# Second and third layer norm of a decoder layer: one square root a pair of tiles on ScalarE, reciprocal and refining step on VectorE

## The chip, the cores and the metric

The kernel runs on one core of a Trainium2 chip. The metric is the device time of one execution in microseconds (us); lower is better. The time before is 491.82 us, the median of 3 runs (491.54 to 492.5).

## What is computed

One decoder layer on x of 4 x 256 tokens and 512 features, in fp32, with a context of 4 x 64 tokens. Each of three blocks ends in a layer norm without weights:

```
layernorm(x) = (x - mean(x)) / sqrt(var(x) + 1e-5)          # over the 512 features

x = layernorm(x + gelu(x @ ((w1.T @ w2.T) * sparse_mask) + b2))
x = layernorm(x + cross_attention(x, ctx))                   # 32 query heads, 8 key/value heads, width 128, rotary positions
x = layernorm(x + (x @ W.T + b) + lora(x))                   # 8 experts of rank 16, weighted per batch by a softmax
```

The router that weights the experts takes the mean of the tokens 107 to 254 of the second norm's output, one row of logits per batch.

## The kernel before

The 1024 tokens are 8 tiles of 128 tokens (X[:, t, :], t = 0 to 7), the tokens on the partitions. Products are taken in three fp32r matmuls each: every operand is split into a high part (a copy on ScalarE, the helpers that end in `_hi`, L801) and a low part (the difference, on VectorE, L1139, or GpSimd, the helpers that end in `_lo`).

Cross attention runs over the 8 key/value heads g (LAST = 7), each with 4 query heads. A head has four units u; `scores`, `mask_scores`, `row_max`, `shift`, `exps`, `row_sum`, `row_inverse`, `probs` (GpSimd, L1728), `probs_transpose`, `pt_hi` and `pt_lo` are the steps of a unit's softmax in that order, over TensorE, VectorE, ScalarE and GpSimd. `value_out(g, n, b)` with `vw_hi` and `vw_lo` multiplies values by the output weights into PSUM bank b; `attend(g, t)` multiplies the probabilities of tile t with them, and `accumulate(g, t)` adds the result to X (L1314). `query`, `q_copy`, `q_cos`, `q_sin` and `q_rot` make the rotated queries. `weight_transpose(j)`, `f_hi(j)` and `f_lo(j)` prepare the weights of the last block.

The order of work is written out by hand, one list for each engine: a loop over the heads 1 to 6, and before and behind it straight lists. An engine takes its list in order; a step that waits for a semaphore holds all that stands behind it on its engine. The change lies in the straight list behind the loop, which begins at some 370 us.

Second norm, tile pair m (tiles 2m and 2m+1): `stats` (L1187, L1189, VectorE) gives mean and variance of a tile, `guess` (L1196 to L1203, VectorE, four steps on 128x2) a first value of 1/sqrt by an integer trick, `newton` on GpSimd three refining steps of four instructions each (L1707 to L1713), `mean_shift` on GpSimd two more (L1758, L1760) that make -mean/deviation, `normalize` on ScalarE (L926) scales and shifts the tile. Then `x2_tile` (TensorE, L267) transposes it, `x2_hi` and `x2_lo` split it, and `base(t)`, `lora_in`, `logits`, `route_transpose` and `lora_out(t)` compute the last block.

Third norm: `out_add(t)` (VectorE, L1378) adds the block's result to X, then come the same `stats`, `guess`, `newton` and `mean_shift`; the last pair has its Newton steps on VectorE (`out_last`, L1215, L1218). `out_scale(m)` on ScalarE (L951) scales the tiles, but tile 6 is scaled on VectorE (L1387), and SyncE stores each tile once it is done.

The first norm lies before the attention. It isn't touched, and its Newton steps stay on GpSimd and VectorE.

Of the kernel before, what the change touches and what calls it, by code (L numbers as in the profile page):

```python
# [31 lines left out]
def decoder_layer(nc, x, ctx_in, amask, w1, w2, b2, smask, wq, wk, wv, wo, fW, fb, fA, fB, rW, rb, rope, out):  # L32
# [24 lines left out]
    with ExitStack() as es:  # L57
# [38 lines left out]
        NM = sb("NM", [P, NT])  # L96
        VH = sb("VH", [P, NT])
# [15 lines left out]
        at_mm at_masked at_hi at_lo_even at_lo_odd y_mm gelu_done x_added ln_stats ln_mean ln_guess ln_newton ln_out ln_shift last_shift out_done out_even  # L113
# [27 lines left out]
        def n_unit(g, u):  # L141
            return UNITS * g + u + 1
# [16 lines left out]
        def x2_bank(t):  # L159
            return (5, 4, 3, 4, 3, 5, 3, 5)[t]  # L160
# [23 lines left out]
        def fy_bank(t):  # L184
            return (0, 6, 2, 7, 1, 3, 6, 7)[t]
# [8 lines left out]
        F_BANKS = (3, 0, 2, 1, 2, 1, 2)  # L194
# [63 lines left out]
        def _(pe):  # L258
# [386 lines left out]
            probs_transpose(LAST - 1, 1)  # L645
            pe.wait_ge(sm["s_sub"], n_unit(LAST - 1, 1))
            score_pair(LAST - 1, 3)
            pe.wait_ge(sm["q_rot"], n_rot(LAST - 1, 3, 0))
            values(LAST)
            pe.wait_ge(sm["vw_lo"], n_vw(LAST - 1, 5))  # L650
            value_out(LAST - 1, 7, 7)
            pe.wait_ge(sm["q_rot"], n_rot(LAST - 1, 3, 1))
            query(LAST, 0, 1)
# [4 lines left out]
            pe.wait_ge(sm["x_added"], n_added(LAST - 1, 0))  # L658
            attend(LAST - 1, 2)
# [4 lines left out]
            pe.wait_ge(sm["x_added"], n_added(LAST - 1, 2))  # L664
            probs_transpose(LAST - 1, 3)
# [3 lines left out]
            query(LAST, 1, 1)  # L669
            pe.wait_ge(sm["x_added"], n_added(LAST - 1, 1))  # L670
            value_out(LAST, 0, 3)
            pe.wait_ge(sm["pt_lo"], n_unit(LAST - 1, 3))
            attend(LAST - 1, 3)
            pe.wait_ge(sm["q_rot"], n_rot(LAST, 0, 0))
            query(LAST, 2, 0)
            pe.wait_ge(sm["s_sub"], n_unit(LAST, 0))
            scores(LAST, 1)
# [12 lines left out]
            pe.wait_ge(sm["vw_lo"], n_vw(LAST, 2))  # L690
            value_out(LAST, 3, 7)
            pe.wait_ge(sm["vw_lo"], n_vw(LAST, 1))
            attend(LAST - 1, 6)
            pe.wait_ge(sm["x_added"], n_added(LAST - 1, 5))
            attend(LAST - 1, 7)
            pe.wait_ge(sm["x_added"], n_added(LAST - 1, 6))
            weight_transpose(0)
            pe.wait_ge(sm["s_sub"], n_unit(LAST, 1))
            scores(LAST, 2)
            pe.wait_ge(sm["q_rot"], n_rot(LAST, 1, 0))  # L700
            query(LAST, 3, 0)
            pe.wait_ge(sm["x_added"], n_added(LAST - 1, 7))
            probs_transpose(LAST, 1)
            pe.wait_ge(sm["f_lo"], 1)
            value_out(LAST, 4, 3)
            pe.wait_ge(sm["q_rot"], n_rot(LAST, 2, 1))
            query(LAST, 3, 1)
            pe.wait_ge(sm["vw_lo"], n_vw(LAST, 3))
            probs_transpose(LAST, 2)
            pe.wait_ge(sm["pt_lo"], n_unit(LAST, 1))  # L710
            attend(LAST, 0)
            pe.wait_ge(sm["q_rot"], n_rot(LAST, 2, 0))
            weight_transpose(1)
# [36 lines left out]
            pe.wait_ge(sm["f_lo"], 4)  # L750
            weight_transpose(5)
            pe.wait_ge(sm["x_added"], n_added(LAST, 6))
            x2_tile(2)
            pe.wait_ge(sm["f_lo"], 5)
            weight_transpose(6)
            pe.wait_ge(sm["x_added"], n_added(LAST, 7))
            base(1)
            pe.wait_ge(sm["tr_lo"], 20)
            x2_tile(3)
            pe.wait_ge(sm["f_lo"], 7)  # L760
            base(2)
            pe.wait_ge(sm["tr_lo"], 21)
            x2_tile(4)
            pe.wait_ge(sm["tr_lo"], 19)
# [3 lines left out]
            pe.wait_ge(sm["tr_lo"], 23)  # L768
            x2_tile(6)
            pe.wait_ge(sm["tr_lo"], 24)  # L770
            x2_tile(7)
            pe.wait_ge(sm["vw_lo"], n_vw(LAST, 7))
            base(3)
            pe.wait_ge(sm["tr_lo"], 26)
            logits()
            pe.wait_ge(sm["tr_lo"], 25)
            lora_in(1)
            pe.wait_ge(sm["lg_step"], 1)
            route_transpose()
            pe.wait_ge(sm["f_lo"], 6)  # L780
# [1122 lines left out]
```

## Time and profile before

| | |
|---|---|
| median of 3 runs | 491.82 us |
| profiled execution, its own time | 492.99 us |
| its span, first to last instruction | 491.2 us |
| TensorE matmul busy | 473.9 us (96%) |
| VectorE busy | 408.3 us (83%) |
| ScalarE busy | 260.6 us (53%) |
| GpSimd busy | 273.4 us (56%) |
| mean granted TensorE clock | 0.985 of full speed |

The profiled execution took 1.17 us more than the median of the runs, and 1.8 us more than its own span. Busy time is the time in which an engine had an instruction under way; matmuls overlap one another, so that a busy TensorE isn't one at its peak. PE is TensorE, PEld its weight loads, DVE VectorE, ACT ScalarE, POOL GpSimd, SP SyncE. Times in the rows are from the span's start.

### The profile page before, as it was taken

How to read it: one execution, taken by the hardware profiler on the slowest of the kernel's cores; microseconds unless marked ns; L12 is line 12 of the kernel's file. 1: busy time of each engine (PE TensorE's matmuls, PEld its weight loads, DVE VectorE, ACT ScalarE, POOL GpSimd, SP SyncE). 2: the span in 40 equal slices, each digit the busy share in tenths (PEclk: the TensorE clock that was granted, in tenths of full speed). 3: DMA queues.
4: the chain of work that ended last, by engine and by line, in shares of the span. 5: the costliest groups of instructions: out<-in, count | busy, mean ns of one | idle time of the engine just before them, and what ended most of it. 6: DMA issues, size and time to landing. Idle time of an engine off the chain costs nothing.

```text
span 491.2 us, 11126 instructions
## 1 busy us (share of the span) xinstructions
PE 473.9 (96%) x4189; PEld 395.9 (81%) x4189; DVE 408.3 (83%) x739; ACT 260.6 (53%) x462; POOL 273.4 (56%) x347
## 2 busy tenths in 40 slices
PE   8999999999999999999999999999999999879991
PEld 8888778888888888888888888888888788668781
DVE  2779898988987898798979987988799889988585
ACT  4574447735673566365735663575458254353423
POOL 3477637854674467456636672676366423156523
PEclk9999999999999999999999999999999999979996
DMA  8943300240023011402040212022002400000013
GB/s 274 353 146 93 124 1 1 87 130 1 2 85 128 0 22 63 128 0 80 7 127 0 85 34 94 0 85 85 0 0 87 67 1 2 1 0 2 0 40 133
DMA packets 29137, 31.56 MB, mean 64 GB/s; under 512 B 6321, under 2 KB 16817, under 8 KB 29114
## 3 DMA queue, kind: packets, MB, share of 16 engines
q1 hardware_dynamic: 29114, 31.25, 20.1%
q8 instruction: 15, 0.25, 0.2%
q14 instruction: 8, 0.07, 0.0%
HBM read 29.15 MB, written 2.10 MB: 64 GB/s over the span
## 4 chain that ended last, share of the span: by engine, by line
PE 77%; DVE 9%; SPq 4%; POOL 3%; issue 3%; DMA 2%; ACT 1%; ACTq 0%; POOLq 0%; DVEq 0%
PE bank L261 23%; PE bank L263 22%; PE bank L262 22%; PE bank L369 6%; PE bank L393 3%; SPq L205 2%; DMA WQr<-in_L_xattn_wq_dram 2%; DVE X L1223 1%; DVE BST L1187 1%; PE bank L267 1%; POOL NW L1711 1%; DVE VWl L1139 1%; POOL NW L1709 1%; POOL RS L1713 1%; POOL NW L1707 1%
## 5 line engine op out<-in xcount | busy, mean ns | idle before, releaser
L1722 POOL TENSOR_TENSOR QS<-QS,SIN 128x512 f32<-128x512 f32 x64 | 83.0, 1297 | 124.4 <-ACT QS L801 124.4
L261 PE MATMUL bank<-XTh,WQh 128*128 128x512 f32 x256 | 101.7, 397 | 0.7 <-DVE XTl L1139 0.7
L263 PE MATMUL bank<-XTh,WQl 128*128 128x512 f32 x256 | 100.0, 391 | 0.0
L262 PE MATMUL bank<-XTl,WQh 128*128 128x512 f32 x256 | 99.7, 390 | 0.0
L1139 DVE TENSOR_TENSOR VWl<-bank,VWh 64x512 fp32r<-64x512 f32 x128 | 88.0, 688 | 9.3 <-ACT VWh L801 7.4
L801 ACT ACTIVATE QS<-bank 128x512 f32<-128x512 f32 x64 | 38.3, 598 | 103.1 <-PE bank L263 102.6
L801 ACT ACTIVATE VWh<-bank 64x512 fp32r<-64x512 f32 x128 | 75.9, 593 | 23.5 <-PE bank L263 20.9
L1251 DVE TENSOR_TENSOR bank<-bank,COS 128x512 f32<-128x512 f32 x64 | 44.6, 697 | 23.2 <-ACT QS L801 22.6
L261 PEld LDWEIGHTS bank<-XTh,WQh 128*128 128x128 f32 x256 | 48.1, 188 | 11.5 <-issue 1.3
L263 PEld LDWEIGHTS bank<-XTh,WQl 128*128 128x128 f32 x256 | 48.0, 188 | 10.5
L262 PEld LDWEIGHTS bank<-XTl,WQh 128*128 128x128 f32 x256 | 48.1, 188 | 9.5
L261 PE MATMUL bank<-VWh,PTh 128*128 128x512 f32 x128 | 50.9, 398 | 0.4 <-DVE X L1314 0.3
L262 PE MATMUL bank<-VWl,PTh 128*128 128x512 f32 x128 | 50.3, 393 | 0.0
L263 PE MATMUL bank<-VWh,PTl 128*128 128x512 f32 x128 | 50.1, 392 | 0.0
L1314 DVE TENSOR_TENSOR X<-X,bank 128x512 f32<-128x512 f32 x64 | 43.2, 674 | 7.2 <-PE bank L263 6.3
L1698 POOL TENSOR_TENSOR WOl<-WOr,WOh 128x512 fp32r<-128x512 f32 x32 | 41.3, 1291 | 12.1 <-ACT WOh L801 11.6
L1263 DVE TENSOR_TENSOR QR<-bank,QS 128x512 f32<-128x512 f32 x64 | 42.9, 683 | 0.4
L1688 POOL TENSOR_TENSOR WQl<-WQr,WQh 128x512 fp32r<-128x512 f32 x32 | 41.0, 1304 | 2.1 <-ACT WQh L801 2.1
L369 PEld LDWEIGHTS bank<-KK,QR 64*64 64x64 f32 x2048 | 31.6, 135 | 5.9 <-issue 5.8
L1728 POOL TENSOR_TENSOR SM<-SM,RI 128x512 f32<-128x512 f32 x32 | 33.5, 1046 | 3.8 <-DVE RI L1296 3.8
L369 PE MATMUL bank<-KK,QR 64*64 64x64 f32 x2048 | 34.2, 220 | 0.0
L261 PEld LDWEIGHTS bank<-VWh,PTh 128*128 128x128 f32 x128 | 24.3, 190 | 6.0 <-DVE X L1314 1.0
(150 smaller groups left out, 965.1 us busy)
## 6 DMA issues: line engine op xcount, KB each, us to landing
WQr<-in_L_xattn_wq_dram SPq DMA_DIRECT2D x8, 1024.0 KB, 5.5
WOr<-in_L_xattn_wo_dram SPq DMA_DIRECT2D x8, 1024.0 KB, 5.4
KVr<-in_L_xattn_wk_dram SPq DMA_DIRECT2D x8, 256.0 KB, 5.4
KVr<-in_L_xattn_wv_dram SPq DMA_DIRECT2D x8, 256.0 KB, 5.5
out_dram<-X SPq DMA_DIRECT2D x8, 256.0 KB, 2.0
X<-in_x_dram SPq DMA_DIRECT2D x3, 512.0 KB, 9.9
WQr<-in_L_attn_w_dram SPq DMA_DIRECT2D x4, 256.0 KB, 4.9
WOr<-in_L_attn_w_dram SPq DMA_DIRECT2D x4, 256.0 KB, 5.1
```

Of the source, the lines that this page charges most:

```text
L261: pe.matmul(o, lh, rh, start=start, stop=False)
L262: pe.matmul(o, lh, rl, start=False, stop=False)
L263: return pe.matmul(o, ll, rh, start=False, stop=stop)
L369: m = pe.matmul(s_tiles(u)[part, a, t, :], QR[head, u % 2, f, t * P + part.start:t * P + part.stop], KK[head, b, f, :], start=f == 0, stop ...
L801: return act.activation(o, i, ACT.Copy)
L1139: return dve.tensor_tensor(o, i, f32(hi), ALU.subtract)
L1251: dve.tensor_tensor(q, q, by_pos(COS, 2, S), ALU.mult).then_inc(sm["q_cos"], 1)
L1263: dve.tensor_tensor(QR[:, u % 2, f, :], bank[:, q_bank(u, f), :], QS[:, u % 2, 1 - f, :], ALU.add if f else ALU.subtract).then_inc(sm["q_r ...
L1314: dve.tensor_tensor(X[:, t, :], X[:, t, :], bank[:, A_BANKS[t], :], ALU.add)\
L1688: pool.tensor_tensor(wq_split(WQl, h), wq_head(WQr, h), f32(wq_split(WQh, h)), ALU.subtract)\
L1698: pool.tensor_tensor(WOl[:, h, :], WOr[:, h, :], f32(WOh[:, h, :]), ALU.subtract)\
L1722: pool.tensor_tensor(q, q, SIN[:, :].unsqueeze(1).broadcast_to([P, 2, S]), ALU.mult)\
```

## The change

For the second and third norm, and for each pair of tiles, `guess`, `newton` and `mean_shift` are replaced. ScalarE computes sqrt(var + eps) of both tiles in one instruction (`std_first`). VectorE takes its reciprocal r, refines it once, r * (1.5 - 0.5 * (var + eps) * r * r), and makes -mean * r, five steps that each need the one before (`std_step`). The third norm's last pair is done like the others. GpSimd has no step of these two norms left; it sets the constant EPS at the start. The order of all four engines' lists behind the loop over the heads is new, with other PSUM banks for some transposes, for some `value_out` and for `base`. The order inside the loop and before it stays.

```diff
+            def std_first(k, m):
+                pair, n = slice(2 * m, 2 * m + 2), 4 * (k - 1) + m
+                act.wait_ge(sm["ln_mean"], NT * k + 2 * m + 2)
+                act.wait_ge(sm["eps_set"], 1)
+                act.activation(RS[:, pair], MV[:, pair, 1], ACT.Sqrt, bias=EPS[:, 0:1]).then_inc(sm["ln_first"], 1)
...
+            def std_step(k, m):
+                pair, n = slice(2 * m, 2 * m + 2), 4 * (k - 1) + m
+                mean, var, r, w = MV[:, pair, 0], MV[:, pair, 1], RS[:, pair], NW[:, pair]
+                dve.wait_ge(sm["ln_first"], n + 1)
+                dve.reciprocal(r, r).then_inc(sm["ln_step"], 1)
+                dve.wait_ge(sm["ln_step"], 5 * n + 1)
+                dve.scalar_tensor_tensor(out=w, in0=r, scalar=-0.5, in1=r, op0=ALU.mult, op1=ALU.mult).then_inc(sm["ln_step"], 1)
+                dve.wait_ge(sm["ln_step"], 5 * n + 2)
+                dve.scalar_tensor_tensor(out=w, in0=var, scalar=LN_EPS, in1=w, op0=ALU.add, op1=ALU.mult).then_inc(sm["ln_step"], 1)
+                dve.wait_ge(sm["ln_step"], 5 * n + 3)
+                dve.scalar_tensor_tensor(out=r, in0=w, scalar=1.5, in1=r, op0=ALU.add, op1=ALU.mult).then_inc(sm["ln_step"], 1)
+                dve.wait_ge(sm["ln_step"], 5 * n + 4)
+                dve.scalar_tensor_tensor(out=NM[:, pair], in0=mean, scalar=-1.0, in1=r, op0=ALU.mult, op1=ALU.mult)\
+                    .then_inc(sm["ln_step"], 1)
...
-            def mean_shift(k, m):
...
             def normalize(k, t):
-                act.wait_ge(sm["ln_shift"], 2 * (t // 2 + 1))
+                act.wait_ge(sm["ln_step"], 5 * (t // 2 + 1))
```

TensorE's new list from the last `scores` on, as far as the second norm reaches (the waits left out; the number behind `value_out` is its bank), beside the old one:

```
old: scores(LAST,3) attend(3) value_out(5) value_out(6) weight_transpose(2) value_out(7) weight_transpose(3)
     probs_transpose(LAST,3) x2_tile(0) x2_tile(1) weight_transpose(4) attend(4) base(0) attend(5) attend(6) attend(7)
new: value_out(5) ... scores(LAST,3) value_out(6, bank 3) attend(3) value_out(7, bank 3, waits for vw_lo(6))
     probs_transpose(LAST,3) weight_transpose(2) x2_tile(0) weight_transpose(3) weight_transpose(4) attend(4)
     x2_tile(1) attend(5) attend(6) base(0) attend(7)
```

VectorE's, from the last `mask_scores`:

```
old: mask_scores(3) stats(1,1) row_max(3) accumulate(3) shift(3) guess(1,0) vw_lo(5) row_sum(3) f_lo(2) row_inverse(3)
     vw_lo(6) stats(1,2) vw_lo(7) f_lo(3) pt_lo(3) x2_lo(0) stats(1,3) accumulate(4) guess(1,1)
new: mask_scores(3) pt_lo(2) row_max(3) accumulate(3) shift(3) vw_lo(6) row_sum(3) std_step(1,0) row_inverse(3)
     stats(1,2) vw_lo(7) stats(1,3) pt_lo(3) f_lo(2) x2_lo(0) accumulate(4) f_lo(3) std_step(1,1)
```

ScalarE's, from `pt_hi(LAST, 2)`:

```
old: pt_hi(2) f_hi(1) vw_hi(5) exps(3) f_hi(2) vw_hi(6) vw_hi(7) f_hi(3) normalize(1,0) normalize(1,1) pt_hi(3)
new: pt_hi(2) std_first(1,0) vw_hi(6) exps(3) vw_hi(7) normalize(1,0) normalize(1,1) pt_hi(3) f_hi(2) x2_hi(0) f_hi(3)
     std_first(1,1)
```

The third norm on VectorE and ScalarE:

```diff
             out_add(0)
             out_add(1)
             stats(2, 0)
+            out_add(2)
             stats(2, 1)
-            guess(2, 0)
-            out_add(2)
+            out_add(3)
             stats(2, 2)
-            out_add(3)
+            stats(2, 3)
             out_add(4)
-            stats(2, 3)
+            std_step(2, 0)
+            stats(2, 4)
+            std_step(2, 1)
             out_add(5)
-            stats(2, 4)
-            guess(2, 1)
             stats(2, 5)
             out_add(6)
-            guess(2, 2)
+            std_step(2, 2)
             stats(2, 6)
             out_add(7)
             stats(2, 7)
-            guess(2, 3)
-            out_last()
+            std_step(2, 3)
+            out_by_dve(6)
...
+            std_first(2, 0)
+            std_first(2, 1)
             out_scale(0)
             out_scale(1)
+            std_first(2, 2)
             out_scale(2)
+            std_first(2, 3)
             out_scale(3)
```

## Rows read from the trace of the kernel before

**Rows 1.** The page's first part: busy time, share of the span, instructions.

```profile
PE 473.9 (96%) x4189; PEld 395.9 (81%) x4189; DVE 408.3 (83%) x739; ACT 260.6 (53%) x462; POOL 273.4 (56%) x347
```

**Rows 2.** Waits of TensorE from 365 to 480 us: in total, times, longest.

```profile
PE bank L393 <- POOL SM L1728: 2.3, 1, 2.3
PE bank L261 <- DVE VWl L1139: 1.7, 1, 1.7
```

**Rows 3.** Half-microsecond stretches: length, busy time of each engine, granted clock, DMA.

```profile
432.00:432.50 0.50, 0.00 (x0) 0.00 (x0) 0.50 (x1) 0.47 (x2) 0.41 (x3) 0.90 0.00 0
...
438.50:439.00 0.50, 0.50 (x3) 0.40 (x2) 0.00 (x0) 0.00 (x0) 0.00 (x0) 0.50 0.00 0
```

**Rows 4.** The chain that ended last, 437 to 440 us: start, duration.

```profile
437.27 0.43 PE bank L261
...
439.38 0.23 PE bank L263
```

**Rows 5.** Timeline, all engines, from the third norm's first sum to its last scale.

```profile
468.27 1.28 DVE L1378 TENSOR_TENSOR X<-X,bank 128x512 f32<-128x512 f32 x2
...
480.65 0.39 PE L263 MATMUL bank<-WOh,PTl 128*128 128x512 f32 x1
...
481.08 0.69 DVE L1378 TENSOR_TENSOR X<-X,bank 128x512 f32<-128x512 f32 x1 [0.47 <-PE bank L263]
...
485.25 0.46 DVE L1215 TENSOR_SCALAR NW<-RS,VH 128x1 f32<-128x1 f32 x2 [1.85 <-POOL RS L1713]
...
487.61 0.81 ACT L951 ACTIVATE X<-X,NM,RS 128x512 f32<-128x512 f32 x1 [0.26 <-DVE NM L1386]
```

**Rows 6.** Timeline, 423 to 434 us: start, duration, engine, line, operation, idle before.

```profile
423.32 1.16 PE L369 MATMUL bank<-KK,QR 64*64 64x64 f32 x64
...
424.63 0.69 DVE L1275 SCALAR_TENSOR_TENSOR bank<-bank,MSK 128x512 f32<-128x512 f32 x1
...
425.23 0.68 DVE L1187 BATCH_NORM_STATS2 BST<-X 128x6 f32<-128x512 f32 x1
...
426.05 0.66 DVE L1280 TENSOR_REDUCE MX<-bank 128x8 f32<-128x512 f32 x1
...
427.15 1.19 ACT L801 ACTIVATE VWh<-bank 64x512 fp32r<-64x512 f32 x2 [5.88 <-PE bank L263]
...
427.82 0.16 DVE L1196 TENSOR_SCALAR VE<-MV 128x2 f32<-128x2 f32 x1
...
428.08 0.17 DVE L1200 TENSOR_SCALAR RS<-VE 128x2 int32<-128x2 int32 x1
428.28 0.17 DVE L1203 TENSOR_SCALAR RS<-RS 128x2 int32<-128x2 int32 x1
...
428.48 1.39 DVE L1139 TENSOR_TENSOR VWl<-bank,VWh 64x512 fp32r<-64x512 f32 x2
428.53 0.19 POOL L1707 TENSOR_TENSOR NW<-RS 128x2 f32<-128x2 f32 x1 [8.15 <-DVE RS L1203]
...
431.23 0.19 DVE L1296 RECIPROCAL RI<-SU 128x8 f32<-128x8 f32 x1
...
432.44 1.04 POOL L1728 TENSOR_TENSOR SM<-SM,RI 128x512 f32<-128x512 f32 x1
...
433.63 1.08 PE L393 MATMUL bank<-ID,SM 128*128 128x128 f32 x4 [2.30 <-POOL SM L1728]
```

**Rows 7.** Timeline of ScalarE at two table loads and at the router's exp.

```profile
25.24 1.28 ACT L836 ACT_TABLE_LOAD   x1
26.53 0.58 ACT L836 ACTIVATE bank<-bank 128x512 f32<-128x512 f32 x1
...
71.60 1.28 ACT L897 ACT_TABLE_LOAD   x1
73.24 0.63 ACT L897 ACTIVATE SM<-SM 128x512 f32<-128x512 f32 x1 [0.36 <-DVE SM L1287]
...
462.21 0.21 ACT L931 ACTIVATE LG<-LG 4x8 f32<-4x8 f32 x1 [3.18 <-DVE LG L1353]
```

More of the change, by code:

```diff
@@ L663, in _ @@
             probs_transpose(LAST - 1, 2)
-            pe.wait_ge(sm["x_added"], n_added(LAST - 1, 2))
-            probs_transpose(LAST - 1, 3)
+            pe.wait_ge(sm["x_added"], n_added(LAST - 1, 0))
+            attend(LAST - 1, 2)
             pe.wait_ge(sm["s_sub"], n_unit(LAST - 1, 3))
@@ L669, in _ @@
             query(LAST, 1, 1)
+            pe.wait_ge(sm["x_added"], n_added(LAST - 1, 2))
+            probs_transpose(LAST - 1, 3)
+            pe.wait_ge(sm["q_rot"], n_rot(LAST, 0, 0))
+            query(LAST, 2, 0)
+            pe.wait_ge(sm["pt_lo"], n_unit(LAST - 1, 3))
+            attend(LAST - 1, 3)
+            pe.wait_ge(sm["s_sub"], n_unit(LAST, 0))
+            scores(LAST, 1)
             pe.wait_ge(sm["x_added"], n_added(LAST - 1, 1))
             value_out(LAST, 0, 3)
[L672 to L677, printed above, removed]
             pe.wait_ge(sm["pt_lo"], n_unit(LAST - 1, 2))
-            probs_transpose(LAST, 0)
-            pe.wait_ge(sm["vw_lo"], n_vw(LAST, 0))
-            value_out(LAST, 1, 3)
+            value_out(LAST, 1, 7)
             pe.wait_ge(sm["x_added"], n_added(LAST - 1, 3))
             attend(LAST - 1, 4)
-            pe.wait_ge(sm["pt_lo"], n_unit(LAST, 0))
-            value_out(LAST, 2, 7)
             pe.wait_ge(sm["q_rot"], n_rot(LAST, 1, 1))
@@ L689, in _ @@
             attend(LAST - 1, 5)
-            pe.wait_ge(sm["vw_lo"], n_vw(LAST, 2))
-            value_out(LAST, 3, 7)
             pe.wait_ge(sm["vw_lo"], n_vw(LAST, 1))
+            probs_transpose(LAST, 0)
+            pe.wait_ge(sm["vw_lo"], n_vw(LAST, 0))
             attend(LAST - 1, 6)
@@ L769, in _ @@
             x2_tile(6)
+            pe.wait_ge(sm["f_lo"], 6)
+            base(2)
             pe.wait_ge(sm["tr_lo"], 24)
             x2_tile(7)
-            pe.wait_ge(sm["vw_lo"], n_vw(LAST, 7))
+            pe.wait_ge(sm["pt_lo"], n_unit(LAST, 2))
             base(3)
+            pe.wait_ge(sm["tr_lo"], 25)
+            logits()
             pe.wait_ge(sm["tr_lo"], 26)
-            logits()
-            pe.wait_ge(sm["tr_lo"], 25)
             lora_in(1)
```

299 lines of the change are left out of this document (139 added, 160 removed).

## Prediction

> **What bounds the kernel now.** I read the page first, then the waits of TensorE, then stretches of the last 70 us, then single engines there. TensorE is busy 96% of the span and VectorE 83% [rows 1]; the reader is to see that a change off TensorE pays only where TensorE waits, or after its last matmul. TensorE's waits from 365 us to 480 us are few: 2.3 us for the last probabilities (L1728 on GpSimd), 1.7 us for VWl, and a third far shorter [rows 2]. Both long ones lie between the last scores (423.32) and the last transpose of probabilities, `probs_transpose(LAST, 3)`, at 433.63. The granted clock is 0.90 of full in 432.0 to 432.5 and 0.50 in 438.5 to 439.0 [rows 3]: TensorE fell to 1.2 GHz while it had no matmul to run. At that level the chain has matmuls 0.43 us apart, and 0.23 from 439.38 on [rows 4]. From 433.63 to 439.3, 5.6 us, it worked at half speed, so 2.8 us are lost. After the last matmul (480.65, ends 481.04) a chain of small work runs to 488.42, the end of the last scale [rows 5].
>
> What stands behind the first long stretch: on GpSimd twelve Newton steps and the mean shift of tile pair 0 start at 428.53, and `probs(LAST, 3)` stands behind them until 432.44, although its reciprocal was done at 431.42 [rows 6]. In the tail VectorE's own Newton of the last pair waits 1.85 us for GpSimd's of the pair before (485.25), and the last scale starts at 487.61 [rows 5].
>
> **The change, its small parts.** It removes from the second and third norm, per pair, 4 VectorE steps and 14 GpSimd steps, and adds one Sqrt on ScalarE and 5 dependent VectorE steps. A dependent small VectorE step starts 0.20 us after the one before (428.08, 428.28) [rows 6]; the reciprocal of 8 elements takes 0.19, so a `std_step` is 5 x 0.20 = 1.0 us, 0.35 more of VectorE than `guess` (427.82 to 428.45). No row shows Sqrt or the fused form on 128x2. The nearest for Sqrt are the 4x8 exp, 0.21, and, for what per-partition operands add, the scale, 0.81, beside a plain exp of as many elements, 0.63 [rows 5, 7]: I take 0.3 and keep 0.2 to 0.5. For a fused step I keep 0.17 to 0.25. The memset of EPS falls at the very start, where GpSimd still waits for the first weights to come from memory: nothing; without that cover, one small step once.
>
> **Table loads.** Exp and Sqrt alternate on ScalarE: Sqrt of pair 0, the last exp, Sqrt of pair 1, the router's exp, Sqrt of the third norm: five new loads if the two functions share no table. A load takes 1.28 us. At 71.60 it started while VectorE was still making what the exp waited for, and the exp followed at 73.24, with that work [rows 7]: it ran ahead of the wait. At 25.24 the Gelu followed at 26.53, 1.29 after the load began [rows 7]. I take 1.28 us each, hidden where ScalarE idles. Idle ScalarE is there: 5.88 us before 427.15 for the first pair, 3.18 before the router's exp [rows 6, 7], and more before the third norm's scales. If it were not hidden it would cost 1.28 each. `std_first` has two waits, and the load may stand behind the first; that bound is in the walk below.
> The Trainium skill (ScalarE: Activation LUTs, What ACT_TABLE_LOAD costs) gives the same 1283 ns and a drain of about 1380 ns more at every switch. The trace disagrees as far as it goes: at 25.24 no such gap stands before or behind the load. By the page my gain would be some 2 us smaller (rival 2). Its rule to do all of one function before the other (Table sets: the hidden batching unit) speaks against this order, in which Sqrt of pair 0 stands ahead of the last exp.
>
> **Second norm, a walk through the new queues.** Prices, from rows: a VectorE 128x512 step starts 0.60 after an independent one (424.63, 425.23), 0.70 after one that it needs; `vw_lo` 1.4; stats 0.8 (425.23 to 426.05); GpSimd's probabilities 1.05; `vw_hi` 1.2; on TensorE at full clock 0.23 a matmul of 512 columns, so 0.69 a `value_out` (3), 1.37 an `attend` (6), and about 0.44 a block of four transposes [rows 4, 6]. Up to `scores(LAST, 3)` I find no longer wait in the new order: TensorE ends it at 424.4 (before: 424.49), with `value_out(LAST, 5)` already done, which before followed it. VectorE has by then taken on one `vw_lo` and one stats and given `pt_lo(2)` away.
> From there, VectorE: stats(1,1) ends 425.0, mask 425.6, pt_lo(2) 426.2, max 426.8, accumulate(3) 427.4, shift 428.0, vw_lo(6) 429.4, row_sum 430.1, std_step(1,0) 431.1, reciprocal 431.3; GpSimd, now free, 431.35 to 432.4; transpose at 432.5. ScalarE: load of the Sqrt table from 424.0, Sqrt at 425.3 to 425.6, vw_hi(6) 426.8, load of the Exp table 428.1, exp 428.8, before row_sum wants it. If both loads stood behind their waits (425.0 and 428.0), the exp would end at 430.0 and the transpose be 0.6 later.
> TensorE: value_out(6) and attend(3) fill 424.4 to 426.45, then `value_out(LAST, 7)`, in bank 3, waits for vw_lo(6) until 429.4, and the transpose until 432.5. So the last transpose is 433.63 - 432.5 = 1.1 us earlier, but two weight transposes (2 x 0.44 = 0.9) that covered the old wait now come after it: 0.2 us gained. Idle time is 2.95 + 2.4 = 5.35 us against 4.0 in the two long waits before and some tenths beside them, so I let the clock fall again for as long. Behind it I find one new wait: attend(5) for accumulate(4), 0.2 to 0.3 us. Everything later (base, lora_in, logits) has the same matmuls, and VectorE stays ahead. The `std_step` of pair 1 to 3 and their Sqrts end over 1 us before the transposes that want their tiles. Second norm: 0, with 2 us to either side for what a walk of two full queues can miss, and 2.8 to gain if the clock holds.
>
> **Third norm.** TensorE ends at 481.04 again (same matmuls, and base(6), base(7) wait for sums long made). VectorE starts out_add(0) at 468.27 [rows 5] and by the prices above is never idle: 7 adds at 0.62, 7 stats at 0.81, 3 std_steps at 1.0, 13.0 us, to 481.25; then out_add(7) to 481.95, stats to 482.8. ScalarE scales tiles 4 and 5 from 480.5 to 482.0, so it is free: Sqrt to 483.15; std_step to 484.2; last scale, 0.81, to 485.05. Before it ended at 488.42 [rows 5]. That is 3.35 earlier: the 1.85 us wait on GpSimd goes, and from 485.25 to 487.61 a Newton and a shift take 2.36 us where Sqrt and std_step take some 1.4; the rest is lost and won in hops of a tenth. The stores behind it are alike, 2.8 us to the span's end, since tiles 6 and 7 follow each other as closely as before. With fused steps at 0.25, the gain is 3.35 - 0.75 - 0.25 = 2.3; with the add unhindered at 481.08, 3.5.
>
> **Sum.** 3.3 + 0 = 3.3 us off 492.99, the profiled execution's own time (span 491.2 and 1.8 around it): 489.7. The median of the runs is 491.82, 1.17 below it, and the same 3.3 off gives 488.5.
>
> **Rivals.**
> 1. The clock does not fall, or for less. The idle second norm is dominated by VectorE's queue; were vw_lo(6) 1 us earlier, value_out(7) would split the idle time more evenly. For it: before, the clock held through the first wait of 1.7 us and fell only in the second. Against: 5.35 us of idle in my walk. Gain 2.8 more: 485.7.
> 2. A switch costs more than its load: ScalarE held as long again (2 x 1.28) each time. Sqrt of pair 0 at 426.9, vw_hi(6) 428.1, exp 431.3, row_sum 432.0, transpose 434.4, 1.9 us late: 490.4. Against it are the loads at 25.24 and 71.60 [rows 7].
> With the 1.38 us of drain that the Trainium skill gives (ScalarE: Activation LUTs, What ACT_TABLE_LOAD costs) it would be 490.6.
> 3. Slower: between `scores(LAST, 3)` and the last transpose all of TensorE stands behind one VectorE queue of ten steps, now holding vw_lo(6) and std_step(1,0) ahead of the reciprocal, with only 2.75 us of matmuls ahead of the transpose in place of 4.3. Every us that mask, exp or Sqrt is late there is a us of idle TensorE. From 3.3 us late (435.8) nothing is gained, from 4.3 (436.8) it is over 0.2% slower: 492.9 or more. For it: VectorE is busy 83% of the span [rows 1] and more than that here. Against: before, this queue ran to its reciprocal at 431.23 with about as much in it [rows 6].
> 4. The tail does not shorten: Sqrt of a pair stands behind ScalarE's scales of the pair before, VectorE behind Sqrt, and out_add(7) behind both. If each of four pairs waits 0.6 us, 2.4 of 3.3 is gone: 490.9 to 491.5, within 0.2%.
>
> **Chances.** The forecast 0.58 (own range 487.3 to 489.8), rival 1 0.12, rival 2 0.10 (a fifth of it within 0.2%), rival 3 0.10, rival 4 0.10. Differences below 0.2%, 1.0 us, can't be told from none. Faster 0.58 + 0.12 + 0.08 = 0.78, same 0.12, slower 0.10. The range 485.6 to 491.0 takes in rivals 1 and 2 and leaves out rival 3 and half of 4.
>
> **What would show it.** Five more ACT_TABLE_LOAD rows of 1.28 us, none on TensorE's waits; std_step rows 0.20 apart; the last transpose of probabilities near 432.5, its wait on L1728 with VectorE's reciprocal just before; TensorE waiting for VWl some 3 us ahead of it; a granted clock of 0.5 for 6 to 7 us; the last matmul within 0.5 us of 481; and 4.0 us, not 7.4, from it to the last scale's end. The prediction is wrong if the last matmul moves by over 2 us either way, or if VectorE's add of tile 7 starts over 0.7 us after its matmul.

## The result, and the profile after

The changed kernel takes 491.05 us (median of 10 executions, 489.74 to 491.75) beside 492.39 us for the kernel before on the same chip (10 executions, 491.54 to 493.05): ratio 0.9973, 95% interval [0.9964, 0.9981]. It is faster, by 0.9 to 1.8 us, where 3.3 us were forecast: 491.05 lies just above the range, which ended at 491.0. Run once more (the control below), it gave 0.9971 [0.9959, 0.9983].

The profiled execution of the changed kernel took 490.72 us, with a span of 488.9. The page's first part, busy time of each engine, its share and its instructions:

```profile
PE 474.7 (97%) x4189; PEld 395.6 (81%) x4189; DVE 409.8 (84%) x733; ACT 269.2 (55%) x475; POOL 253.7 (52%) x250
```

Beside [rows 1], GpSimd has 97 instructions fewer and ScalarE's busy time is 8.6 us longer: five more table loads (6.4 us) and eight Sqrt. TensorE's busy time is alike, VectorE's 1.5 us longer.

The waits of TensorE from 365 to 482 us, as total, times, longest:

```profile
PE bank L262 <- DVE VWl L1152: 2.8, 1, 2.8
PE bank L394 <- POOL SM L1751: 1.1, 1, 1.1
PE bank L268 <- ACT X L934: 0.5, 1, 0.5
PE bank L262 <- DVE X L1343: 0.3, 1, 0.3
PE bank L262 <- DVE XTl L1152: 0.3, 1, 0.3
```

Beside [rows 2] the wait for VWl is longer (2.8, not 1.7), the one for the last probabilities shorter (1.1, not 2.3). Two are new, of 0.5 and 0.3 us: for X from ScalarE's `normalize` (L934), and for XTl. These two are what the prediction said would not exist. The one for X from VectorE (L1343) is the wait of `attend(5)` for `accumulate(4)`, which the walk had foreseen.

The stretch that answers to [rows 6], on the timeline of all engines (start, duration, engine, line, operation, idle time before it and its releaser):

```profile
424.95 1.28 ACT L930 ACT_TABLE_LOAD   x1
...
426.25 0.30 ACT L930 ACTIVATE RS<-MV,EPS 128x2 f32<-128x2 f32 x1
...
427.65 1.28 ACT L898 ACT_TABLE_LOAD   x1
...
429.04 1.38 DVE L1152 TENSOR_TENSOR VWl<-bank,VWh 64x512 fp32r<-64x512 f32 x2
429.16 0.63 ACT L898 ACTIVATE SM<-SM 128x512 f32<-128x512 f32 x1 [0.23 <-DVE SM L1316]
...
430.48 0.79 PE L262 MATMUL bank<-WOh,VTh 128*128 128x512 f32 x1 [2.81 <-DVE VWl L1152]
...
430.94 0.15 DVE L1239 RECIPROCAL RS<-RS 128x2 f32<-128x2 f32 x1
...
431.12 0.16 DVE L1241 SCALAR_TENSOR_TENSOR NW<-RS 128x2 f32<-128x2 f32 x1
...
431.79 0.20 DVE L1325 RECIPROCAL RI<-SU 128x8 f32<-128x8 f32 x1
...
432.06 1.04 POOL L1751 TENSOR_TENSOR SM<-SM,RI 128x512 f32<-128x512 f32 x1 [9.74 <-DVE RI L1325]
...
433.25 1.09 PE L394 MATMUL bank<-ID,SM 128*128 128x128 f32 x4 [1.12 <-POOL SM L1751]
```

The last scores end at 425.39. Sqrt's table is loaded in 1.28 us right behind ScalarE's last use of the old one and Sqrt starts at its end; the exp's load runs at 427.65 while VectorE still makes what the exp wants, and the exp follows 0.23 us behind the end of its load, with VectorE's shift. Small dependent VectorE steps are 0.20 apart. TensorE's second wait ends in the order that the walk gave: sum, `std_step(1,0)`, reciprocal, GpSimd, and then the last transposes, which are those of the probabilities (L394).

The granted clock there, in half-microseconds (length, busy time by engine, clock, DMA), answering to [rows 3]:

```profile
430.00:430.50 0.50, 0.02 (x1) 0.02 (x1) 0.50 (x2) 0.00 (x0) 0.00 (x0) 0.51 0.00 0
...
436.00:436.50 0.50, 0.50 (x5) 0.50 (x4) 0.50 (x2) 0.43 (x2) 0.31 (x1) 0.50 0.00 0
436.50:437.00 0.50, 0.50 (x5) 0.50 (x4) 0.50 (x2) 0.24 (x2) 0.50 (x1) 0.66 0.00 0
```

TensorE fell to 1.2 GHz before `value_out(LAST, 7)` had its VWl and was back at 2.4 GHz at 436.8, after 6.8 us.

The tail, answering to [rows 5]:

```profile
482.00 0.39 PE L264 MATMUL bank<-WOh,PTl 128*128 128x512 f32 x1
...
482.42 0.69 DVE L1407 TENSOR_TENSOR X<-X,bank 128x512 f32<-128x512 f32 x1 [0.19 <-PE bank L264]
...
484.09 0.29 ACT L930 ACTIVATE RS<-MV,EPS 128x2 f32<-128x2 f32 x1 [1.12 <-DVE MV L1202]
484.42 0.17 DVE L1239 RECIPROCAL RS<-RS 128x2 f32<-128x2 f32 x1 [0.36 <-ACT RS L930]
...
485.40 0.81 ACT L956 ACTIVATE X<-X,NM,RS 128x512 f32<-128x512 f32 x1 [1.01 <-DVE NM L1247]
```

The last matmul ends at 482.39, VectorE's last addition starts with it, and the last scale ends at 486.21: a tail of 3.82 us where it was 7.38. That is 3.56 us gained at the very end, while the last matmul comes 1.35 us later than in the kernel before.

### The profile page after: what moved, and what is told of

It reads as the page before. It is cut to its first block, busy times and chain, and to the rows that moved or that the text cites. A ratio compares the mean times of both kernels' runs of the same rounds, so it can differ in the third digit from the quotient of the medians.

```text
span 488.9 us, 11036 instructions
## 1 busy us (share of the span) xinstructions
PE 474.7 (97%) x4189; PEld 395.6 (81%) x4189; DVE 409.8 (84%) x733; ACT 269.2 (55%) x475; POOL 253.7 (52%) x250
## 4 chain that ended last, share of the span: by engine, by line
PE 83%; DVE 12%; POOL 2%; ACT 1%; issue 1%; POOLq 0%; DVEq 0%; ACTq 0%
PE bank L262 24%; PE bank L264 23%; PE bank L263 23%; PE bank L370 7%; PE bank L394 3%; DVE VWl L1152 2%; DVE X L1252 1%; DVE BST L1200 1%; PE bank L283 1%; PE bank L268 1%; DVE X L1343 1%; DVE XTl L1152 1%; DVE QR L1186 1%; DVE bank L1280 1%; PE bank L427 0%
## 5 line engine op out<-in xcount | busy, mean ns | idle before, releaser
L1280 DVE TENSOR_TENSOR bank<-bank,COS 128x512 f32<-128x512 f32 x64 | 44.6, 697 | 20.9 <-ACT QS L802 20.4
L1343 DVE TENSOR_TENSOR X<-X,bank 128x512 f32<-128x512 f32 x64 | 42.9, 672 | 6.1 <-PE bank L264 5.2
L262 PE MATMUL bank<-WOh,VTh 128*128 128x512 f32 x64 | 26.9, 421 | 2.8 <-DVE VWl L1152 2.8
```

What stands on the lines that cost most here:

```text
L262: pe.matmul(o, lh, rh, start=start, stop=False)
L1280: dve.tensor_tensor(q, q, by_pos(COS, 2, S), ALU.mult).then_inc(sm["q_cos"], 1)
L1343: dve.tensor_tensor(X[:, t, :], X[:, t, :], bank[:, A_BANKS[t], :], ALU.add)\
```

## The experiments

All ratios are to the kernel before, timed beside the experiment. For reading the traces I use four lengths: A, from the end of the last scores to the end of the last matmul; in it the idle time of TensorE, and the matmul time lost to 1.2 GHz (busy time by one minus the granted clock, summed over quarter-microsecond stretches from 425 to 445 us); and B, the tail from the last matmul to the end of the last scale. The profiled executions:

| kernel | end of last scores | A | idle in A | lost to 1.2 GHz | low clock lasted | B |
|---|---|---|---|---|---|---|
| before | 424.49 | 56.55 | 4.26 | 2.79 | 6.8 | 7.38 |
| changed | 425.39 | 57.00 | 5.05 | 2.62 | 6.8 | 3.82 |
| changed, control | 424.57 | 58.12 | 5.74 | 2.96 | 6.8 | 3.82 |
| e1 third norm only | 424.30 | 56.74 | 4.30 | 2.97 | 6.8 | 5.50 |
| e2 second norm only | 425.27 | 56.95 | 5.05 | 2.54 | 6.8 | 8.56 |
| e3 changed, no bias | 424.90 | 55.55 | 4.96 | 1.57 | 3.4 | 3.82 |
| e4 reciprocal first | 424.90 | 56.70 | 5.17 | 1.64 | 3.4 | 3.83 |
| e5 fill | 424.75 | 55.85 | 2.17 | 0 | 0 | 3.82 |
| e6 late bias | 425.93 | 55.95 | 4.29 | 2.80 | 6.8 | 3.83 |
| e7 three edits | 424.97 | 55.42 | 1.94 | 0 | 0 | 3.82 |
| e8 before, fill | 424.62 | 54.87 | 1.34 | 0 | 0 | 7.33 |
| e9 late bias, reciprocal first | 425.14 | 55.40 | 4.43 | 1.62 | 3.4 | 3.82 |
| e10 third norm, new order | 424.42 | 56.25 | 4.23 | 2.47 | 6.8 | 3.83 |
| e11 before, no bias | 424.70 | 55.34 | 4.23 | 1.57 | 3.4 | 7.32 |

What the clock does differs between executions, and is to be kept apart from what an edit does. The low clock lasted 6.8 us in some profiled executions and 3.4 us in others, which is worth 1.0 to 1.4 us of matmul time, and it began at 430.01 in one execution of the changed kernel and at 431.51 in the other. No kernel was profiled with both lengths; that one kernel has both is inferred from the mean granted clocks of its timed executions (see the control, c1), and from e3 and e11, whose profiles have no new wait of TensorE in that stretch and yet half its length.

A steadier length leaves the clock out. All kernels have the same lists up to the loop's last `scores` (348.53 in the kernel before, the first fence; 348.71 in the changed one, the second); behind it they differ. The last `scores` of all start at 424.23 in the changed kernel.

```profile
348.53 2.09 PE L369 MATMUL bank<-KK,QR 64*64 64x64 f32 x128
```

```profile
348.71 2.10 PE L370 MATMUL bank<-KK,QR 64*64 64x64 f32 x128
...
424.23 1.16 PE L370 MATMUL bank<-KK,QR 64*64 64x64 f32 x64
```

Let M be the time from the start of the loop's last `scores` to the start of the last transposes of probabilities, and N the time from there to the end of the last matmul, less what 1.2 GHz cost in it. From M nothing is taken off: it is 84.53 us both in the changed kernel and in the control, though the low clock began 1.5 us apart in them.

| kernel | loop's last scores to end of last scores | M | lost to 1.2 GHz behind M | N | M + N |
|---|---|---|---|---|---|
| before | 75.96 | 85.10 | 2.80 | 44.6 | 129.7 |
| e10, e11 | 75.91, 75.93 | 85.05, 85.07 | 2.47, 1.57 | 44.6 | 129.7 |
| changed, control | 76.68, 76.67 | 84.53 | 1.80, 2.95 | 47.3 | 131.9, 131.8 |
| e4 reciprocal first | 76.67 | 83.81 | 1.64 | 47.9 | 131.7 |
| e3, e6 (no adds, late adds) | 76.67, 76.66 | 84.53, 84.52 | 1.57, 1.98 | 46.1 | 130.6 |
| e9 late bias, reciprocal first | 76.67 | 83.81 | 1.63 | 46.6 | 130.4 |

Executions of kernels with the same walk agree within 0.1 us in M + N (e1 has 129.7 too, e2 131.9), so differences of some tenths can be read from it.

### e1 and e2: each norm by itself

e1 is the kernel before with the third norm's new steps and VectorE's new queue there; e2 is the changed kernel with the third norm's old steps and VectorE's old queue.

```diff
# e1, TensorE's order as before
             out_add(1)
             stats(2, 0)
+            out_add(2)
             stats(2, 1)
-            guess(2, 0)
-            out_add(2)
+            out_add(3)
...
+            std_step(2, 3)
+            out_by_dve(6)
```

> The kernel before with the new third norm alone (std_first, std_step, the new order of the last sums), the second norm and all orders ahead of it as before. Theory T (two parts of opposite sign: the tail gains 3.5 us, the second norm's new order loses 1.3): last matmul near 481.0 as before, 3.8 us from its end to the end of the last scale in place of 7.4, time 3.4 to 3.6 us below the kernel before, ratio 0.993. Rival R (the tail's gain is smaller in most executions than in the profiled one, and the second norm costs nothing): ratio 0.997, as the whole change.

> The changed kernel with the old third norm (guess, Newton steps on GpSimd, mean shift, the last pair's Newton on VectorE, old order of the last sums). Theory T: last matmul 1.2 to 1.4 us later than in the kernel before, tail of 7.4 us behind it, time 1.2 to 1.5 us above the kernel before, ratio 1.003. Rival R: ratio 1.000.

e1: 490.51 us, ratio 0.9961 [0.9947, 0.9975], less gain than expected. e2: 495.91 us, 1.0072 [1.0058, 1.0086], more loss. Their sum does not give the change, because the tail's queues depend on each other. In e1 VectorE wants `out_add(2)` before its matmuls are issued (TensorE had `lora_out(2)` behind `base(5)`); VectorE's timeline:

```profile
472.24 0.69 DVE L1403 TENSOR_TENSOR X<-X,bank 128x512 f32<-128x512 f32 x1 [1.87 <-PE bank L264]
...
482.77 0.67 DVE L1403 TENSOR_TENSOR X<-X,bank 128x512 f32<-128x512 f32 x1
```

It stands still for 1.87 us, is never ahead again, and starts the last addition at 482.77, 1.7 us after the last matmul (481.04): a tail of 5.50. In e2 the mirror of it costs 1.61 us at 478.18, and the last Newton waits 2.39 us for GpSimd's. The prediction's tail had counted on a VectorE that "is never idle", and that held only with TensorE's new order, which the prediction had as given and did not count as part of the gain. So e1 and e2 don't price the two norms; e10 does it.

### e10: the third norm with the order that it needs

```diff
# e10 = e1, and on TensorE (with the banks of the changed kernel)
             base(4)
             lora_out(0)
             lora_out(1)
+            lora_out(2)
+            lora_out(3)
             pe.wait_ge(sm["ts_out"], 2)
             base(5)
-            lora_out(2)
-            lora_out(3)
             lora_out(4)
-            lora_out(5)
-            pe.wait_ge(sm["fy_out"], 2)
+            pe.wait_ge(sm["fy_out"], 1)
             base(6)
+            lora_out(5)
             lora_out(6)
-            pe.wait_ge(sm["fy_out"], 4)
+            pe.wait_ge(sm["fy_out"], 2)
             base(7)
```

> The kernel before with the new third norm and with TensorE's order and banks of the last stage as the changed kernel has them (lora_out(2) and (3) ahead of base(5)); the second norm is the old one. Theory T: the tail needs the new order of TensorE as well; VectorE no longer waits at its third sum, last matmul to last scale is 3.8 to 4.0 us instead of 5.5, and with the last matmul at 481.0 the span is 487.6 to 487.9, the time 488.9 to 489.2 (ratio 0.993). Rival: the old order further ahead (x2, lora_in) makes VectorE late for out_add(0) by itself; then the tail stays at 5.5 and the time at 490.5.

488.9 us (488.52 to 489.13), ratio 0.9926 [0.9912, 0.9939]: 3.0 to 4.3 us faster than before, 3.4 by the medians. Its timeline at the end:

```profile
480.28 0.39 PE L264 MATMUL bank<-WOh,PTl 128*128 128x512 f32 x1
...
480.70 0.69 DVE L1403 TENSOR_TENSOR X<-X,bank 128x512 f32<-128x512 f32 x1 [0.18 <-PE bank L264]
...
482.37 0.29 ACT L930 ACTIVATE RS<-MV,EPS 128x2 f32<-128x2 f32 x1 [1.12 <-DVE MV L1198]
...
483.69 0.81 ACT L956 ACTIVATE X<-X,NM,RS 128x512 f32<-128x512 f32 x1 [1.02 <-DVE NM L1243]
```

The last matmul ends at 480.67 and the tail is 3.83. The third norm's term is settled: 3.35 forecast, 3.4 measured. And it says what the rest of the change costs: 491.05 - 488.9 = 2.15 us for the second norm and the queues around it (the control, timed beside e10, took 491.06). The medians alone would be weak for this, since 3 of e10's 5 executions had a mean granted clock of 0.995 and only 4 of the changed kernel's 19. But M + N, in which the clock has no part, says the same: 131.85 - 129.7 = 2.15 us.

### e3 and e11: without the bias adds

The new waits point at the `std_step` of pairs 2 and 3. VectorE's and GpSimd's timelines in the changed kernel:

```profile
447.26 0.16 DVE L1239 RECIPROCAL RS<-RS 128x2 f32<-128x2 f32 x1
447.45 1.06 DVE L1241 SCALAR_TENSOR_TENSOR NW<-RS 128x2 f32<-128x2 f32 x1
448.55 1.22 DVE L1243 SCALAR_TENSOR_TENSOR NW<-MV,NW 128x2 f32<-128x2 f32 x1
449.80 0.16 DVE L1245 SCALAR_TENSOR_TENSOR RS<-NW,RS 128x2 f32<-128x2 f32 x1
...
452.81 0.15 DVE L1239 RECIPROCAL RS<-RS 128x2 f32<-128x2 f32 x1
453.00 0.21 DVE L1241 SCALAR_TENSOR_TENSOR NW<-RS 128x2 f32<-128x2 f32 x1
453.24 1.22 DVE L1243 SCALAR_TENSOR_TENSOR NW<-MV,NW 128x2 f32<-128x2 f32 x1
```

```profile
447.20 2.54 POOL L1780 TENSOR_TENSOR X<-X,WOr 128x512 f32<-128x512 f32 x2 [6.59 <-PE bank L268]
451.93 2.52 POOL L1780 TENSOR_TENSOR X<-X,WOr 128x512 f32<-128x512 f32 x2 [2.18 <-PE bank L268]
```

A step of two elements a partition took 1.06 and 1.22 us instead of 0.16, and each ended with one of GpSimd's bias adds (two of 1.27 us from 447.20, two from 451.93). The reciprocals, with one input, were not held; the held ones have two inputs in SBUF. So `std_step(1,2)` took 2.9 us and `std_step(1,3)` 2.0 instead of 1.0. ScalarE's `normalize` waited for them, and TensorE for it:

```profile
450.19 1.52 ACT L934 ACTIVATE X<-X,NM,RS 128x512 f32<-128x512 f32 x2 [1.52 <-DVE NM L1247]
```

```profile
451.15 0.63 PE L268 MATMUL bank<-ID,X 128*128 128x128 f32 x4 [0.47 <-ACT X L934]
...
453.00 0.47 PE L262 MATMUL bank<-XTh,WOh 128*128 128x512 f32 x1 [0.29 <-DVE XTl L1152]
```

The Trainium skill (SBUF — State Buffer, Who interferes with whom) has this rule: a VectorE instruction with two SBUF inputs contends with a GpSimd instruction that reads SBUF, and the one that comes second is blocked for the whole of the other. The rows agree, with 1.06 and 1.22 us against 0.16. The prediction did not weigh it.

```diff
# e3 = changed kernel; e11 = kernel before; in both the bias stays out of the output
-            add_bias(0)
...
-            add_bias(7)
...
-                dve.wait_ge(sm["bias_in"], t + 1)
```

> The changed kernel without the eight adds of the last block's bias on GpSimd (the bias is left out of the result). Theory G (the small steps of std_step that read two operands from SBUF are held while GpSimd adds the bias: 1.06 and 1.22 us in place of 0.16 for pair 2, 1.22 for pair 3, 0.46 for pair 1): std_step of pairs 1 to 3 takes 1.0 us each (before: 1.2, 2.9 and 2.0), the waits of 0.47 and 0.29 us at x2_tile and lora_in go, last matmul 1.0 to 1.3 us earlier, ratio to the kernel before 0.9947 in place of 0.9973. Rival V (VectorE's queue is late there by itself, since its sums came late from TensorE at half clock): the steps shorten, the last matmul moves by under 0.4 us, ratio 0.997.

> The kernel before with the eight bias adds left out (the output lacks the bias). Leaving them out of the changed kernel brought its last matmul 1.45 us nearer to the last scores and gave 0.9952 of before against 0.9973. Theory C: the change itself exposed TensorE to the bias adds, since before it the refining ran on GpSimd, in turn with the adds; then the kernel before gains at most 0.4 us (ratio 0.9992 to 1.0), last matmul 56.2 to 56.6 us after the last scores. Rival: the kernel before paid for them just as much, and the loss is no part of the change; then the last matmul is 55.1 to 55.5 us after the last scores, and the ratio about 0.997.

e3: 489.87 us, 0.9952 [0.9938, 0.9965], and both waits (0.47, 0.29) are gone. A is 1.45 us shorter than in the changed kernel, but this execution's low clock lasted only 3.4 us: 1.05 of the 1.45 is clock. It was also 0.67 us longer idle before the last transposes. With both taken out, 1.45 - 1.05 + 0.67, the adds cost 1.1 us; by M + N it is 1.2.

e11: 491.93 us, 0.9993 [0.9984, 1.0002]: the kernel before does not gain by it. The expectation's length would have said the opposite (A is 55.34, 1.2 us shorter, in the rival's range), but the table shows all of that in the clock (1.57 lost instead of 2.79) and the same idle time, 4.23 beside 4.26. So the contention is a cost of the change: before, the refining ran on GpSimd in turn with the adds, and VectorE had only its guess to be held (1.14 us once, beside an add), off TensorE's path.

### e6: the same sum, with the adds later

```diff
             def add_bias(t):
                 pool.wait_ge(sm["tr_mm"], 18 + t + 1)
+                if t > 0:
+                    pool.wait_ge(sm["ln_step"], 10 if t == 1 else 20)
```

> The changed kernel with the bias adds of tiles 1 to 7 kept back on GpSimd by one more wait: tile 1 until std_step of pair 1 is done, tiles 2 to 7 until that of pair 3. Nothing is left out. Theory G (the adds hold the small steps): std_steps of 1.0 us each, TensorE's waits for X (L934) and XTl gone, last matmul 1.0 to 1.4 earlier, ratio 0.995, as without the adds. Rival (the adds, now packed from 451 us on, hold other small steps, those of the mean and the router): the second waits come back near 460 us and the ratio stays at 0.997.

489.83 us (488.77 to 490.3), 0.9941 [0.9926, 0.9955], with the whole computation. VectorE's steps of pair 2 and GpSimd's adds:

```profile
448.21 0.16 DVE L1241 SCALAR_TENSOR_TENSOR NW<-RS 128x2 f32<-128x2 f32 x1
448.40 0.16 DVE L1243 SCALAR_TENSOR_TENSOR NW<-MV,NW 128x2 f32<-128x2 f32 x1
```

```profile
441.85 1.30 POOL L1782 TENSOR_TENSOR X<-X,WOr 128x512 f32<-128x512 f32 x1 [3.83 <-DVE NM L1247]
452.72 6.31 POOL L1782 TENSOR_TENSOR X<-X,WOr 128x512 f32<-128x512 f32 x5 [9.57 <-DVE NM L1247]
```

No step is held, no wait of TensorE is left behind 440 us, A is 1.05 us shorter with the clock low just as long. By the medians 1.2 of the 2.15 us come back (by the ratios, 0.9941 against 0.9973, 1.6), and by M + N 1.2, to within 0.05 us what leaving the adds out gives in e3.

### e4 and e9: the reciprocal ahead of the refining

```diff
             row_sum(LAST, 3)
-            std_step(1, 0)
             row_inverse(LAST, 3)
+            std_step(1, 0)
```

> The changed kernel with one edit: VectorE takes row_inverse(LAST, 3) ahead of std_step(1, 0). Theory P (TensorE's wait of 1.1 us before the last transpose of probabilities stands behind the 0.9 us of std_step): the transpose starts 0.9 us earlier (432.4), last matmul 0.8 to 1.0 earlier, ratio 0.9955. Rival N (normalize of pair 0 comes 0.1 later and the x2 transposes, VectorE's queue or the clock take it back): transpose earlier, last matmul within 0.3 us, ratio 0.997.

> The changed kernel with bias adds 1 to 7 behind the last refining step and the reciprocal of the last unit ahead of the first std_step, no extra matmuls. Late bias alone gave a last matmul 1.05 us nearer to the last scores and 0.9941, reciprocal first alone 0.3 nearer and 0.9958. If the two add up (theory G with N), the last matmul comes 1.3 to 1.5 us nearer than in the changed kernel, 55.5 to 55.7 us after the last scores, and the time is 489.3 to 489.7. If the fill was what made the three-edit version best (rival), this one is no better than late bias alone, 489.8.

e4: 489.97 us, 0.9958 [0.9944, 0.9971]. e9, with e6's edit as well: 488.9 us (488.59 to 489.8), 0.9931 [0.9917, 0.9945]. The last transposes start 0.7 us earlier, at 7.15 and 7.14 us after the last scores instead of 7.86, but most of that is lost again behind them: N grows by 0.6 in e4 and by 0.5 in e9. M + N falls by only 0.1 us (e4 beside the changed kernel, hardly beyond its spread) and 0.2 us (e9 beside e6). So rival N holds. In e9's trace `std_step(1,0)` now runs beside the probabilities on GpSimd, and is held again:

```profile
431.06 0.16 DVE L1241 SCALAR_TENSOR_TENSOR NW<-RS 128x2 f32<-128x2 f32 x1
431.07 1.06 POOL L1751 TENSOR_TENSOR SM<-SM,RI 128x512 f32<-128x512 f32 x1 [9.00 <-DVE RI L1325]
...
431.26 0.89 DVE L1243 SCALAR_TENSOR_TENSOR NW<-MV,NW 128x2 f32<-128x2 f32 x1
...
432.28 0.69 PE L394 MATMUL bank<-ID,SM 128*128 128x128 f32 x4 [1.10 <-POOL SM L1751]
```

The timed gains are 1.1 us (e4 beside the changed kernel) and 0.9 (e9 beside e6), but the executions differ in their mean granted clock. Like with like, they are smaller: at 0.988 to 0.991, 490.8 (2 executions of e4) beside 491.16 (15 of the changed kernel), and 489.44 (2 of e9) beside 490.07 (4 of e6). In both profiled executions the low clock lasted 3.4 us, and began behind `value_out(LAST, 7)` instead of ahead of it; in e9:

```profile
432.50:433.00 0.50, 0.50 (x6) 0.50 (x5) 0.50 (x2) 0.42 (x1) 0.00 (x0) 0.71 0.00 0
...
436.00:436.50 0.50, 0.50 (x4) 0.30 (x2) 0.50 (x2) 0.50 (x1) 0.10 (x1) 0.87 0.00 0
```

So a good part of the timed gain goes with a clock that was low for less time. That the order of the two steps brings this about is what these traces suggest, but e3 has the same short stretch with the order of the changed kernel, so it isn't shown.

### e5, e7 and e8: TensorE kept busy

Seventeen matmuls of 512 columns whose result nobody reads, 12 ahead of `value_out(LAST, 7)` and 5 behind it; e7 is that with the edits of e6 and e4; e8 puts 16 of them into the two waits of the kernel before.

```diff
+            fill(1, 12)
             pe.wait_ge(sm["vw_lo"], n_vw(LAST, 6))
             value_out(LAST, 7, 3)
+            fill(1, 5)
```

> The changed kernel with 17 matmuls of 512 columns that nobody reads, 12 ahead of value_out(LAST, 7) and 5 behind it, in TensorE's two waits, into a free bank. Theory C (the clock falls because TensorE is idle there for 2.8 us and 1.1 us, and the low level costs 2.6 us, half of the 5.3 us of matmuls that run at it): the granted clock stays at 1.00 from 426 to 440 us, the last matmul 2.2 to 2.6 us earlier, ratio to the kernel before 0.9925. Rival V (VectorE's queue is as tight as TensorE there): the clock stays up, but waits of TensorE for VectorE's sums after the last transpose grow by over half of it, ratio 0.995 to 0.997.

> The changed kernel with the filling matmuls, the late bias adds and row_inverse ahead of std_step(1, 0) together. If the three costs are separate (2.4 + 1.1 + 0.4 to 0.9 us): ratio 0.989 to 0.990. If VectorE bounds the stretch once TensorE is quick: 0.992 or more, with TensorE waiting for VectorE's X and XTl between 436 and 456 us.

> The kernel before with 16 such matmuls, 7 ahead of value_out(LAST, 7) and 9 behind weight_transpose(3), in its two waits of 1.7 and 2.3 us. Theory C: the clock stays up, last matmul 2.4 to 2.8 us earlier, ratio 0.9945. If so, the low clock cost both kernels nearly the same, and is no part of the difference between them. Rival: the loss is not the clock's, ratio 1.000.

e5: 489.54 us, 0.9943 [0.993, 0.9956]. e7: 489.1 us, 0.9932 [0.992, 0.9944]. e8: 491.33 us, 0.9976 [0.9967, 0.9984]. In all three the clock stayed at 2.4 GHz through the two waits. It is worth less than the lost time in the table. e5 and e8 get 1.15 us and 1.68 us of A, where 2.62 and 2.79 us of matmul time were lost; of the 2.62, 0.8 lay ahead of the last transposes, where TensorE had to wait anyway, so the 1.15 is to be held against 1.80. Beside the control, e5 gets 2.27 of 2.95. By the medians the fill is worth 1.5 us (e5) and 1.2 us (e8). In e5 one new wait is for PTl (0.3), in e8 one of 0.8, in e7 these:

```profile
PE bank L432 <- DVE VWl L1160: 0.7, 1, 0.7
PE bank L262 <- DVE PTl L1160: 0.6, 1, 0.6
```

TensorE at full speed runs into VectorE's queue, which is as long as before. And e7 is no better than e9, which has no fill (489.1 and 488.9, intervals overlapping): once the adds are out of the way, what the fill saves is mostly waited for again.

### c1: the changed kernel once more

> The changed kernel once more, unaltered. The first comparison gave 0.9973 [0.9964, 0.9981], 1.34 us, where the two profiled spans differ by 2.3. If the two profiled executions happened to lie apart from their medians (theory S, spread between executions), the ratio is 0.997 again, 490.9 to 491.3 us. If instead the first comparison was the odd one (theory P, the profiles tell the true difference), the ratio is near 0.9953, 490.1 us.

491.06 us (9 executions), 0.9971 [0.9959, 0.9983]; theory S holds. Its trace shows how far two executions of one kernel lie apart: the last scores end 0.82 us earlier, and A is 1.12 longer, with 0.69 more idle time and 0.34 more lost to the clock, because the low stretch began at 431.51, behind `value_out(LAST, 7)`, and so lay more on matmuls and less on waits. Of the 2.3 us between the two profiled spans, 0.6 is that the profiled execution of before lay above its median and 0.3 that the other lay below. The mean granted clock goes with the times of single executions: among 45 timed ones of the kernel before, 22 had 0.985 or 0.986 (median 492.82 us) and 19 had 0.991 (492.08); among 19 of the changed kernel, 15 had 0.988 to 0.990 (491.16) and 4 had 0.995 (median 490.0).

## Why the prediction was wrong

- **Small parts and table loads: right.** Sqrt took 0.29 to 0.30 us (0.3 forecast), a fused step 0.16, 0.20 apart, a load 1.28, five more of them, none in front of TensorE. Nothing else stands at a switch: at 424.95 the load follows the work before it by 0.01 us and Sqrt starts 1.30 after it; at 427.65 the load follows `vw_hi` by 0.02 and the exp 1.51 after it, of which 0.23 is a wait for VectorE. So rival 2 falls. The Trainium skill (ScalarE: Activation LUTs, What ACT_TABLE_LOAD costs) has some 1380 ns of drain at each switch; no switch here shows it.
- **Third norm, -3.35: right.** The tail is 3.82 us (4.0 forecast) and e10 gives 3.4 by the medians, 3.55 by the tails in the traces (7.38 - 3.83), with M + N at 129.7 as before. One condition was unstated: TensorE's new order; without it (e1) only 1.8 us are gained. Rival 4 falls.
- **The first waits of the walk: right in kind.** TensorE waited 2.8 us for VWl (2.95 forecast), and the last transposes started 7.86 us after the last scores (8.1 forecast). That the control had them at 432.43, beside 432.5 in the forecast, is luck: everything in that execution ran 0.8 us ahead of the first profile, which has 433.25. The clock was low for 6.8 us (6 to 7) in both profiles, so rival 1 falls for them. Four of 19 executions had a mean granted clock of 0.995 and a median of 490.0; none of these was profiled. With the clock held by fill (e5) the gain was 1.5 us, not rival 1's 2.8. Rival 3's mechanism, the long VectorE queue, is there, but its price is not 3.3 us.
- **The first step that failed** is the start of the walk: "TensorE ends it at 424.4 (before: 424.49), with `value_out(LAST, 5)` already done, which before followed it." It priced 0.69 us of matmuls ahead of the last scores at nothing. But in the kernel before TensorE was idle for only 0.14 us between 365 us and the end of its last scores, so there was no wait to fill. From the loop's last scores to the end of the last ones it took 76.66 to 76.68 us in nine profiled executions with the new order and 75.91 to 75.96 in five with the old: 0.7 us more. VectorE's queue hangs on those scores (the 7.86 us above), so the last transposes came 0.55 us earlier by M, not 1.1, and with the two weight transposes (0.9) now behind them that is 0.3 us lost where 0.2 was to be gained.
- **The step that cost most** is "The `std_step` of pair 1 to 3 and their Sqrts end over 1 us before the transposes that want their tiles. Second norm: 0". It priced `std_step` at 5 x 0.20 us, everywhere. Where GpSimd adds the bias at the same time, steps with two SBUF inputs are held to the end of an add, and pairs 2 and 3 take 2.9 and 2.0 us; TensorE waits 0.47 and 0.29 us for them and is late in smaller amounts around it. Taking the adds away (e3) or moving them (e6) gives back 1.2 us.
- **The sum for the second norm and the queues** is +2.15 us (0, with 2 us to either side, forecast): 1.2 for the adds, 0.3 for the transposes, 0.34 for the wait of `attend(5)`, which the walk named at 0.2 to 0.3 and left out of its sum, and some 0.25 that no run separates. The last matmul ended at 482.39, where the prediction had it within 0.5 us of 481. In M + N e9 still stands 0.7 us above e10; in the two profiled executions the clock makes up for it (1.63 us lost behind M in e9, 2.47 in e10).
- **The base.** The forecast subtracted 3.3 from a median of 491.82 (three executions); beside the changed kernel the same kernel took 492.39. That made the forecast 0.6 us too low by itself, and with 3.3 - 1.34 = 1.96 us too little gain it is the whole miss of 2.55 us.

The version to keep is e10. e10 and e9 both took 488.9 us, 2.15 below the change, with ratios 0.9926 [0.9912, 0.9939] and 0.9931 [0.9917, 0.9945] to the kernel before; but e10 is the smaller edit, since it leaves the second norm where it was, and its walk without the clock is 0.7 us shorter.

## What to carry to other kernels

Moving small steps from one engine to another changes what they run beside: before pricing a VectorE step from a quiet stretch, list what GpSimd does at that time, and whether the step has two inputs in SBUF. A 0.16 us step can then cost a whole GpSimd instruction (1.3 us here). Price an end section together with the order of every queue that feeds it, and when two traces of one or two microseconds' difference are compared, take the time lost to TensorE's lower clock out of both first, behind the last wait that another engine sets: it differed by over 1 us between executions, and once (e11) it alone would have named the wrong theory. Work that is moved ahead of a point where an engine hardly waits moves that point back by its whole length (0.7 us here), and all that hangs on it.

## What was not expected of the hardware

- VectorE steps of 128x2 with two inputs in SBUF take 0.16 us alone and 1.06, 1.22 and 0.89 us beside a GpSimd instruction of 1.0 to 1.3 us; a reciprocal with one input beside the same instruction takes 0.16. One input is no safeguard for every step: in the kernel before an int32 `tensor_scalar` of the guess (450.73, L1203) took 1.14 us beside an add (450.53, 1.31), and 0.17 in e11 without the adds.
- The stretch at 1.2 GHz lasted 6.8 us in seven of the profiled executions above and 3.4 us in four, for alike idle time of TensorE in A (4.2 to 5.7 us and 4.2 to 5.2), and there was none at all with fill (1.3 to 2.2 us idle). In two executions of one kernel it began 1.5 us apart.
- Taking that stretch away returned only part of the matmul time that it had cost behind the last transposes (1.15 of 1.80 us or, beside the control, 2.27 of 2.95; 1.68 of 2.80 in the kernel before). New waits for VectorE, up to 0.8 us, came in its place.
